# Sums of y's squares for tiles 3 to 6 of each chunk: from a VectorE reduction to four accumulated TensorE products

## The reference

```python
def rmsnorm(y, w):
    return y * jax.lax.rsqrt(jnp.mean(y * y, axis=-1, keepdims=True) + EPS) * w
...
y = jnp.moveaxis(ys, 0, 1).reshape(B, T, H * P)
y = rmsnorm(y, rms_weight)
return y @ out_proj_w.T
```

## Time and profile before

| | |
|---|---|
| median of 3 runs | 606.64 us (604.37 to 607.63) |
| the profiled execution, its own time | 608.52 us |
| its span, first to last instruction | 606.8 us |
| mean granted TensorE clock | 0.966 |
| PE busy | 526.3 us, 87% |
| PEld busy | 437.9 us, 72% |
| DVE busy | 470.1 us, 77% |
| ACT busy | 482.5 us, 80% |
| POOL busy | 433.8 us, 71% |

### The profile page before, as it was taken

The page is one execution under the profiler, slowest core; times in us unless marked ns, Lnnn a source line. Parts: engine busy times, 40 slices in busy tenths (PEclk is TensorE's granted clock), DMA queues, the critical chain, the costliest instruction groups (busy, mean ns, idle before and its releaser), DMA issues. The chain is left out here.

```text
span 606.8 us, 13457 instructions
## 1 busy us (share of the span) xinstructions
PE 526.3 (87%) x3932; PEld 437.9 (72%) x3932; DVE 470.1 (77%) x1093; ACT 482.5 (80%) x1478; POOL 433.8 (71%) x568
## 2 busy tenths in 40 slices
PE   5978999999999898896999888899998786879287
PEld 4866888888887777785887777788777575766175
DVE  6666576687659999983767999997559979953995
ACT  3799999999998879695998887789999789843101
POOL 7348777878777887783678796977768876944742
PEclk9989999999999999997999999999999989987769
DMA  8841222132111112231111111232211112000001
GB/s 198 219 112 50 75 74 81 59 99 76 59 44 52 59 59 59 62 102 35 56 59 59 59 53 31 93 94 93 88 31 54 63 41 66 27 18 2 1 0 36
DMA packets 52309, 39.44 MB, mean 65 GB/s; under 512 B 7301, under 2 KB 48010, under 8 KB 52234
## 3 DMA queue, kind: packets, MB, share of 16 engines
q1 hardware_dynamic: 45898, 35.39, 19.7%
q10 hardware_dynamic: 6336, 3.15, 1.8%
HBM read 33.44 MB, written 4.46 MB: 62 GB/s over the span
## 5 line engine op out<-in xcount | busy, mean ns | idle before, releaser
L937 ACT ACTIVATE turned<-ps,sct 128x128 f32<-128x128 f32 x376 | 110.7, 446 | 0.0
L922 ACT ACTIVATE turned<-ps,sct 128x128 f32<-128x128 f32 x368 | 103.3, 434 | 6.4 <-DMA sct<-packed 3.9
L1282 DVE TENSOR_TENSOR_SCAN lmat<-arow,band 128x512 f32<-128x512 f32 x64 | 86.5, 1356 | 5.6 <-POOL band L651 3.6
L630 POOL TENSOR_TENSOR cn<-turned 128x256 f32<-128x256 f32 x64 | 54.4, 850 | 39.4 <-ACT turned L937 39.4
L1290 DVE TENSOR_TENSOR mmat<-ps,lmat 128x512 f32<-128x512 f32 x64 | 43.9, 685 | 46.4 <-PE ps L1816 46.4
L630 POOL TENSOR_TENSOR bn<-turned 128x256 f32<-128x256 f32 x64 | 52.9, 826 | 36.7 <-PE ps L1848 25.1
L1816 PE MATMUL ps<-cT,bT 128*128 128x128 f32 x512 | 69.4, 278 | 8.2 <-DVE state L1321 5.8
L1816 PEld LDWEIGHTS ps<-cT,bT 128*128 128x128 f32 x512 | 63.2, 191 | 16.4 <-issue 14.9
L828 ACT ACTIVATE area<-ps 128x256 f32<-128x256 f32 (+1 forms) x68 | 34.6, 565 | 42.8 <-PE ps L2049 14.0
L1721 PE MATMUL ps<-w_sel_hi,xt_hi 128*128 128x512 f32 x128 | 59.1, 462 | 1.4 <-ACT turned L937 1.4
L1848 PE MATMUL ps<-wu,bn 128*128 128x128 f32 x384 | 54.6, 286 | 4.0 <-DVE mmat L1290 3.9
(11 more groups left out here) (271 smaller groups left out, 1430.1 us busy)
## 6 DMA issues: line engine op xcount, KB each, us to landing
arow<-alpha_rows SPq DMA_DIRECT2D x32, 512.0 KB, 3.7
drow<-decay_rows SPq DMA_DIRECT2D x64, 128.0 KB, 3.1
area<-in_L_attn_a_x_dram SPq DMA_DIRECT2D x4, 512.0 KB, 6.1
xT_rows<-turned SPq DMA_DIRECT2D x4, 512.0 KB, 4.9
xt<-xT_rows SPq DMA_DIRECT2D x32, 64.0 KB, 2.5
area<-in_L_attn_a_x_dram ACTq DMA_DIRECT2D x6, 256.0 KB, 3.0
out_dram<-area ACTq DMA_DIRECT2D x6, 256.0 KB, 2.4
area<-L_attn_a_sel_proj_w_dram SPq DMA_DIRECT2D x2, 512.0 KB, 6.4
```

The costliest lines, as they stand in the source:

```text
L630: pool.tensor_tensor(out[:, 0], zc[:, 0], zs[:, 1], ALU.subtract)
L922: last = act.activation(dst[h][:, N * q:N * q + N], bank(BK_B)[:, N * q:N * q + N], ACT.Copy, scale=scalars(c, k)[:, at + HH * h + q:at + ...
L937: last = act.activation(dst[h][:, N * q:N * q + N], bank(BK_C)[:, N * q:N * q + N], ACT.Copy, scale=scalars(c, k)[:, at + HH * h + q:at + ...
L1282: dve.tensor_tensor_scan(lmat[h], arow[i2][:, HH * P * h:HH * P * (h + 1)], band[h], 0.0, ALU.mult, ALU.add).then_inc(l_dve, 1)
```

## The change

For tiles 3, 4, 5 and 6 of each chunk (16 of 32), ACT squares `yT` into a buffer of the same plain layout, four blocks one behind the other. DVE's `y_sum` does nothing for these tiles. PE multiplies each of the four blocks by ones and accumulates the four products in PSUM, and `project_out` waits for ACT's square itself (`ysq_act`). The other 16 tiles are computed as before. `ysq` gets two buffers, taken by turns, and ACT waits for PE's `project_out` of two tiles before (`o_pe`), not for DVE's sum of the tile before. Counts on `q_dve` follow `sums_done`, since it now counts half of the tiles.

```diff
--- before.py
+++ after.py
@@ -153,6 +153,14 @@
 ON_VECTOR = [m for m in range(2 * NB) if m not in ON_GPSIMD]
 
 
+SQUARES_ON_PE = (3, 4, 5, 6)
+
+
+def sums_done(c, b):
+
+    return (NB - len(SQUARES_ON_PE)) * c + len([q for q in range(b + 1) if q not in SQUARES_ON_PE])
+
+
 def v_step(name, c):
     return len(VSTEPS) * c + VSTEPS.index(name) + 1
 
@@ -347,7 +355,8 @@
         yinter = sb("yinter", [P, 2 * P])
         yT_both = sb("yT", [P, 8 * P])
         yT = [yT_both[:, 0:4 * P], yT_both[:, 4 * P:8 * P]]
-        ysq = sb("ysq", [P, 4 * P])
+        ysq_both = sb("ysq", [P, 2, 4 * P])
+        ysq = ysq_both[:, 0]
         ysum = sb("ysum", [P, P])
         state = sb("state", [P, NB, H * PD])
 
@@ -954,9 +963,13 @@
             def y_square(c, b):
                 tile = NB * c + b
                 act.wait_ge(y_dve, 2 * tile + 2)
-                after(act, q_dve, tile)
-                act.activation(ysq[:].rearrange("p (t j) -> p j t", j=4), yT[b % 2].rearrange("p (j t) -> p j t", j=4),
-                               ACT.Square).then_inc(ysq_act, 1)
+                after(act, o_pe, tile - 1)
+                own = ysq_both[:, b % 2]
+                if b in SQUARES_ON_PE:
+                    act.activation(own, yT[b % 2], ACT.Square).then_inc(ysq_act, 1)
+                else:
+                    act.activation(own.rearrange("p (t j) -> p j t", j=4), yT[b % 2].rearrange("p (j t) -> p j t", j=4),
+                                   ACT.Square).then_inc(ysq_act, 1)
 
             def f_T_out(c, t):
                 act.wait_ge(f_pe[t % 2], use_done(("T", t), c))
@@ -1324,10 +1337,12 @@
 
             def y_sum(c, b):
 
+                if b in SQUARES_ON_PE:
+                    return
                 tile = NB * c + b
                 dve.wait_ge(ysq_act, tile + 1)
                 after(dve, o_pe, tile)
-                dve.tensor_reduce(ysum[:], ysq[:].rearrange("p (t j) -> p t j", j=4), AX.X, ALU.add).then_inc(q_dve, 1)
+                dve.tensor_reduce(ysum[:], ysq_both[:, b % 2].rearrange("p (t j) -> p t j", j=4), AX.X, ALU.add).then_inc(q_dve, 1)
 
             def o_out(c, b):
                 dve.wait_ge(o_pe, NB * c + b + 1)
@@ -1852,11 +1867,19 @@
             def project_out(c, b, more):
 
                 tile = NB * c + b
-                pe.wait_ge(q_dve, tile + 1)
+                if b in SQUARES_ON_PE:
+                    pe.wait_ge(ysq_act, tile + 1)
+                else:
+                    pe.wait_ge(q_dve, sums_done(c, b))
                 pe.wait_ge(u_act, tile + 3 if more else NT)
                 for j in range(4):
                     pe.matmul(bank(BK_M)[:, 0:D], yT[b % 2][:, P * j:P * j + P], w_out[:, j], start=(j == 0), stop=(j == 3))
-                pe.matmul(bank(BK_M)[:, D:2 * D], ysum[:], ones[:], start=True, stop=True).then_inc(o_pe, 1)
+                if b in SQUARES_ON_PE:
+                    for j in range(4):
+                        last = pe.matmul(bank(BK_M)[:, D:2 * D], ysq_both[:, b % 2, P * j:P * j + P], ones[:], start=(j == 0), stop=(j == 3))
+                else:
+                    last = pe.matmul(bank(BK_M)[:, D:2 * D], ysum[:], ones[:], start=True, stop=True)
+                last.then_inc(o_pe, 1)
 
 
             def f_free(c, use):
```

## The result

| | before | after |
|---|---|---|
| median, 12 runs each on one chip | 605.97 us (602.45 to 608.08) | 600.37 us (595.94 to 601.43) |
| ratio, 95% interval | | 0.9908 (0.9886 to 0.993) |
| the profiled execution: time, span | 608.52, 606.8 us | 600.63, 598.9 us |
| mean granted TensorE clock | 0.966 | 0.974 |

Some executions of a kernel fall in a slower state of the chip, and all medians and ratios here are of the others. A ratio is given with its 95% interval and can differ by 0.3% from the quotient of the two medians.

The account below looks back on a forecast made before the run. The bound changes by tile: ACT and PE in a loop in chunk 0, DVE at tile 4 and ACT at tile 6 of chunk 2. Terms 0.9 + 0.2 + 1.0 = +2.1 us gave 608.7 us, range 604.5 to 612.0.

Parts of the forecast that it names:

- the last sentence's assumption: At the loop's back edge: the engines' common stall taken as unchanged; its moving was listed as proof of being wrong.
- PE's idle time of 2.49 us and its half speed: Chunk 3, tile 3: after this idle time eight matmuls took 1.74 us, so three blocks could cost up to 1.3 us.
- Chunk 0, +0.9: Chunk 0: tiles 3, 4 and 5 each +0.3 us; at tile 6 a PE wait hides the blocks.
- the loop: Chunk 0: PE and ACT wait for each other; each tile puts 0.67 us on and takes 0.38 off, +0.3.
- PE's slack of 0.37 us: Chunk 0: PE alone as the bound has 0.37 us to spare in a tile, so 0.67 - 0.37 gives 0.3.
- Chunks 1 and 2, +0.2: Both loop chunks together: what DVE and ACT win is given back by tile 6, about +0.1 us each.
- DVE's sum at tile 4: Chunks 1 and 2: DVE's 0.60 us won whole, PE's wait falling from 1.88 to about 0.6.
- Chunk 3, +1.0: Chunk 3: +0.67 us at tile 3, -0.60 at tile 4, +0.67 at tile 5, about +0.3 at tile 6.
- PE has room (faster): All chunks: blocks slip between PE's groups, -7.5 us or 599.1; with half of it, about 604, chance together 0.14.
- Its rule: Chunk 0: headroom judged by weight loads, 84% busy, would give PE 1.9 us to spare and hide the blocks.
- The forecast's +2.1: Whole kernel: chunk terms 0.9 + 0.2 + 1.0 us, slower, put on the median of 606.64.

Follow-up runs that it names:

- runs 4 and 9: Kernel before with PE's extra blocks repeated, nothing taken from ACT or DVE: run 4 602.04 us (0.9969); run 9, loop top at offset 32, 602.42 us (0.9963).
- run 1: Kernel before with 48 empty instructions ahead of PE's work: 605.07 us, ratio 1.0002 to before.
- run 5: Kernel before with PE's loop top placed at offset 32 of a 256-instruction block: 597.69 us, ratio 0.9885 to before.
- run 6: Kernel before with PE's loop top placed at offset 244 of a 256-instruction block: 605.31 us, ratio 1.0025 to before.

## Why the prediction was wrong

- **The step that failed is the last sentence's assumption**, that "the engines' common stall at the loop's back edge, which I take as unchanged". It had no row and no price. I had listed it as what would make me wrong, and it did: 6.2 us in the two profiles, 4.5 in the mean over fourteen.
- **The same fault once more at tile 3 of chunk 3.** I read PE's idle time of 2.49 us and its half speed as part of the kernel's work. They were a late load beside an instruction transfer, 2.8 us of the two profiles' difference. ACT's 2.06 us "issue" above it was there to be asked about.
- **Chunk 0, +0.9:** +0.8 measured (+0.30 at tile 3 and +0.48 over tiles 4 to 6), with PE full as forecast. Of its two derivations only the loop is borne out, 0.67 on and 0.38 off. By PE's slack of 0.37 us the blocks alone would have cost 0.3 a tile; they cost 0.60 (11.90 to 12.51). With the blocks alone PE still waits 0.30 us for ACT in a tile (runs 4 and 9), and with the lighter engines alone a tile is 0.37 shorter (11.90 to 11.53), so the slack is a wait for ACT, and moves with ACT.
- **Chunks 1 and 2, +0.2:** DVE's sum at tile 4 is won (-0.46) and given back in tiles 5 to 7 (+0.57): +0.1 for chunk 2, the other columns of chunk 1 alike. PE's wait at tile 4 fell from 1.88 to 1.05, not to 0.6: with the blocks alone it is 1.22 us, with the lighter engines alone 1.72, so what is ahead of it had come early too.
- **Chunk 3, +1.0:** +0.66 at tile 3, +0.50 over tiles 4 to 6.
- **The rival "PE has room (faster)"**, whose time of 599.1 is near the measured one by chance, is wrong in every place: chunk 0 lost, chunk 2 kept nothing. Its rule, that headroom is to be read from the weight loads' share, fails here: PEld was at 84% in chunk 0, and three blocks cost 0.60 of their 0.67 us.
- **The sum and what is left.** The forecast's +2.1 and the +2.0 by stretches agree, and so do the runs with the loop's top held at 32. The medians differ by 5.6 us the other way. With +2.0 for the change and -4.5 for the back edge, 3.1 are left; so are 2.6 of the 7.1 between the kernel before and itself at offset 32. The late load at tile 3 of chunk 3 is of that size (3.4 and 3.0 us over 14.24), and both profiles of PE's stream as it stood before have it (before and run 1), while neither the kernel after nor run 5 has. The drop of the clock at tile 4 is smaller: 0.7 us net (17.0 and 47.4 against 15.67 and 48.0 in chunk 2), in five of twelve tiles with the work of before and in none of sixteen with a shorter wait, so on average some 0.6 us for the two loop chunks, an estimate.
- **Open.** In how many executions of before the load is late was not measured, no run moved the load and the transfer apart by itself, and why the change gains rather than costs at offset 244 (-0.9, against +2.0 by stretches) is not settled. The two profiles can't tell: run 6's is the fastest of its twelve executions.

## What to carry to other kernels

Before a small change is priced in a kernel with a loop, look for idle time of the kind "issue" behind a back edge, and count how the change moves the loop's first instruction: 48 instructions in a part that runs once were worth twice the change's own cost, with the other sign. To judge such a change, hold the loop's place and compare stretches between the same two events rather than whole times. A long idle time that the kernel's own work doesn't explain needs its own cause first, since it may be gone in the changed kernel for a reason that is no part of the change, with the half speed behind it.

## What the runs showed of the hardware

- PE's stream comes in 16 KB transfers of 0.9 to 1.8 us. At the back edge PE stands still for 1.3 to 2.3 us, and with the loop's top at offset 244 of 256 once more, for 1.9 to 2.5 us. At 32 and 128 it doesn't.
- A stand-still costs more than its idle time: two of 2.1 and 2.9 us, in place of one of 1.7, are 3.3 us of idle time and cost 6.2, since the matmuls behind them run at half the clock (0.50 from 280 to 286 us).
- A load of 24 KB (`sct`) lands about 1.8 us after its issue; where a 16 KB instruction transfer of PE's starts 0.65 to 1.17 us behind the issue, it lands after 2.65 to 3.57 us, in ten of ten cases.
- The same idle time does not always bring the same clock: after 2.7 us at the ending's start, the next 13 us had a granted clock of 0.52 to 0.87, and the endings took 62.7 to 65.4 us; after 1.9 us at tile 4, five tiles of twelve had 0.90 and 1.3 us more, seven had 1.00.
- ACT's square of 128 x 512 float32 takes 632 ns into a plain layout (median of 16), and 1218 ns (median of 32 before; 1259 of 16 after) when it writes with a stride of four elements. What it holds ACT for, from its start to the next start, is 0.51 and 0.91 us.
